# Fewer products ahead of the scores, operand loads behind a store, and a last stage entered in another order

## What is computed

```python
x = norm(x + attention0(x))   # 16 heads of dim 8, causal, distance penalty, biases
x = norm(x + experts(x))      # 8 experts, the best one for each token, 128 -> 512 -> 128
x = norm(x + attention1(x))   # 16 heads of dim 64, RMS norms on q and k, gated distance bias
x = norm(x + ffn(x))          # the last stage
# attention1 ends with  y = softmax(scores) @ v;  return y @ Wproj
# ffn: h = silu(x @ w1 * s1) * (x @ w2 * s2); h = gelu(h @ h1 * ..); h = gelu(h @ h2 * ..); return h @ w3 * s3
```

## Time and profile before

| | |
|---|---|
| median of three runs | 2333.69 us |
| profiled execution, as timed | 2337.64 us |
| its span | 2335.9 us |
| TensorE busy | 2102.8 us |
| VectorE busy | 1513.2 us |
| ScalarE busy | 1210.6 us |
| GpSimd busy | 778.7 us |
| TensorE's granted clock, mean | 0.944 of full speed |

### The profile page before, as it was taken

How to read it: one execution, slowest core, us unless ns; L and a number is a source line. 1 busy time by engine, 2 the same in 40 slices (tenths; PEclk the granted TensorE clock), 3 DMA queues, 4 the chain that set the end, 5 groups by cost and what they waited for, 6 DMA issues and landing times.

```text
span 2335.9 us, 33711 instructions
## 1 busy us (share of the span) xinstructions
PE 2102.8 (90%) x11360; PEld 1168.3 (50%) x11408; DVE 1513.2 (65%) x3409; ACT 1210.6 (52%) x1925; POOL 778.7 (33%) x480
## 2 busy tenths in 40 slices
PE   5899999998577999877999999999999995999998
PEld 2333333333566555544555555555555553655644
DVE  3777777773732778865887878888888843323311
ACT  2366666667344678854565556655565641223232
POOL 5000000000501211003777777777777780000000
PEclk7799999999689999976999999999999996999999
DMA  5233333111365579646666656666566666253300
GB/s 171 88 122 123 109 123 123 53 50 30 128 170 156 169 224 295 202 157 152 168 170 157 148 148 170 169 166 155 147 169 166 178 157 182 57 124 82 83 9 9
DMA packets 230043, 318.68 MB, mean 136 GB/s; under 512 B 22300, under 2 KB 152652, under 8 KB 229464
## 3 DMA queue, kind: packets, MB, share of 16 engines
q1 hardware_dynamic: 214568, 288.64, 45.1%
q0 software_dynamic: 7664, 24.39, 2.9%
q10 hardware_dynamic: 7640, 3.48, 0.5%
HBM read 176.52 MB, written 105.84 MB: 121 GB/s over the span
## 4 chain that ended last, share of the span: by engine, by line
PE 29%; DVE 16%; issue 8%; DMA 2%; SPq 0%; ACT 0%; DVEq 0%
PE ps L1242 9%; PE ps L906 4%; DVE a1mx L958 4%; PE ps L890 3%; DVE a1mx L962 3%; PE ps L860 3%; DVE a1KB L972 3%; PE ps L891 3%; PE ps L1193 3%; DVE a1QB L972 3%; DVE a1mx L955 1%; PE ps L1253 1%; PE ps L1231 1%; DMA frec<-s_rec 1%; PE ps L1230 1%
## 5 line engine op out<-in xcount | busy, mean ns | idle before, releaser
L1078 POOL TENSOR_TENSOR a1sum<-a1sum,a1prob 128x1024 f32<-128x1024 f32 (+3 forms) x256 | 489.4, 1912 | 66.5 <-ACT a1prob L1015 35.3
L1015 ACT ACTIVATE a1prob<-ps 128x512 f32<-128x512 f32 (+2 forms) x640 | 325.8, 561 | 251.6 <-PE ps L893 236.3
L461 DVE TENSOR_REDUCE a0grid<-ps 128x8 f32<-128x1024 f32 x288 | 349.2, 1222 | 137.2 <-PE ps L337 74.6
L563 ACT ACTIVATE a0prob<-ps 128x1024 f32<-128x1024 f32 x288 | 292.2, 1025 | 192.0 <-PE ps L363 96.8
L955 DVE CUSTOM_DVE_ANT_0 ps<-ps,c_mask_ij 128x128 f32<-128x128 f32 x496 | 262.6, 551 | 99.3 <-issue 97.6
L890 PE MATMUL ps<-a1QA,a1KA 69*128 69x512 f32 (+3 forms) x768 | 285.2, 379 | 3.4 <-PEq L33 3.4
L906 PE MATMUL ps<-a1prob,a1V 128*64 128x512 f32 (+3 forms) x1536 | 277.2, 504 | 0.0
L860 PE MATMUL ps<-a1KA,a1QA 68*128 68x128 f32 x744 | 240.8, 390 | 27.9 <-DVE a1mx L958 14.7
L891 PE MATMUL ps<-a1QB,a1KB 128*128 128x512 f32 (+3 forms) x768 | 264.2, 351 | 0.0
L906 PEld LDWEIGHTS ps<-a1prob,a1V 128*64 128x64 f32 x1536 | 104.2, 140 | 170.5 <-issue 143.6
L1075 POOL TENSOR_TENSOR a1sum<-a1prob 128x768 f32<-128x768 f32 x64 | 156.2, 2440 | 78.8 <-ACT a1prob L1015 76.7
(11 more groups left out here) (271 smaller groups left out, 3231.2 us busy)
## 6 DMA issues: line engine op xcount, KB each, us to landing
a1FK<-s_k SPq DMA_DIRECT2D x128, 256.0 KB
a1FQ<-s_q SPq DMA_DIRECT2D x128, 256.0 KB
s_xs<-c_zero POOLq DMA_DIRECT2D x19, 1024.0 KB, 9.1
s_q<-mqkT SPq DMA_DIRECT2D x32, 512.0 KB
s_k<-mqkT SPq DMA_DIRECT2D x32, 512.0 KB
s_v<-mv SPq DMA_DIRECT2D x32, 512.0 KB, 4.3
a1V<-s_v SPq DMA_DIRECT2D x32, 512.0 KB, 4.6
a1KA<-a1KB SPq DMA_DIRECT2D x64, 256.0 KB
```

Source lines behind the costliest of these rows:

```text
L461: dve.tensor_reduce(grid[g % 2][:, :, a:b + 1:b - a], banks(("max", k)), axis=AX.X, op=ALU.max).then_inc(s1_free, 1)
L563: act.activation(prob[:, :, a:b + 1:b - a, :], banks(("exp", q)), ACT.Exp).then_inc(p_full, 1)
L1015: act.activation(weights_of(g, u)[:, group[0]:group[-1] + 1, off:BANK], both(e, u, group), ACT.Exp).then_inc(weighed, 1)
L1078: pool.tensor_tensor(t[:, :, off:BANK], t[:, :, off:BANK], weights_of(g, u)[:, :, off:BANK], ALU.add).then_inc(summed, 1)
```

## The change

In the first attention:

- `EARLY` is 13. The last four of the 17 products come in the loop; the wait for drains ahead of the loop covers products 8 to 11.
- `high` and `low` have three buffers each, and there are three `stored` semaphores; ScalarE waits for the store of three chunks before.
- SP issues load_second(0) behind store(2), not ahead of it, and load_first(1) behind store(4), not store(3).
- ScalarE issues BK of group 0 behind its part of products 0 to 7.
- The waits for a batch's stores stand in one helper, ahead of each load.

In the last stage:

- The buffers of the reciprocals are swapped: those of chunk 0 lie where pair 29's operands were. load_rec(0) goes ahead of load_y(0), a pair earlier than before.
- The loads of chunk 2 are issued in `sync_program` behind the last pair's store, ahead of the write of its denominators and of the wait for the inversion.
- VectorE does join(1) ahead of the inversion; inversion and scale(2) come behind chunk 0's gates, join(2) behind chunk 1's.
- TensorE does project(2) at the end of loop 0, not ahead of the first hidden layer. ScalarE's root for join(2) moves to loop 1.

```diff
-    EARLY, NPROD, COL = 17, len(products), dim + 1
+    PARTS3, EARLY, NPROD, COL = 3, 13, len(products), dim + 1
...
-        high, low = ([over(f"{n}{r}", [P, 2, CHUNK], F32R) for r in range(2)] for n in ("high", "low"))
+        high, low = ([over(f"{n}{r}", [P, 2, CHUNK], F32R) for r in range(PARTS3)] for n in ("high", "low"))
...
+        def batch_stored(engine, b):
+
+            for c in range(b * seq // CHUNK, (b + 1) * seq // CHUNK):
+                engine.wait_ge(stored[c % PARTS3], 16 * 4 * (c // PARTS3 + 1))
...
             store(1)
+            batch_stored(sp, 0)
             still(sp, Q[0], "q0", 0, loaded1[0])
-            sp.wait_ge(cleared, 1)
-            load_second(sp, 0)
             for c in range(2, chunks):
                 store(c)
-                if c == 3:
+                if c == 2:
+                    sp.wait_ge(cleared, 1)
+                    load_second(sp, 0)
+                if c == 4:
                     sp.wait_ge(cleared, 2)
                     load_first(sp, 1)
...
-            for n in range(8, EARLY - 3):
-                drained(n)
+            for n in range(8, EARLY - 1):
+                if n % 8 < 2 * RING:
+                    drained(n)
...
-                if c > 1:
-                    act.wait_ge(stored[c % 2], 16 * 4 * (c // 2))
+                if c >= PARTS3:
+                    act.wait_ge(stored[c % PARTS3], 16 * 4 * (c // PARTS3))
...
-            for n in range(6, EARLY - 1):
+            for n in range(6, 8):
                 drain(n)
             act.wait_ge(cleared_first, 1)
+            batch_stored(act, 0)
             moving(act, BK[0], "k0", 0, loaded1[0])
-            for n in range(EARLY - 1, NPROD):
+            for n in range(8, NPROD):
                 drain(n)
...
+                if g == G:
+                    load_y(2)
+                    load_rec(2)
+                    load_x(2)
                 if g > 0:
                     store_den(g - 1)
...
-        rec = [[over(f"rec{r}{q}", [P, 4, CHUNK], place) for q, place in enumerate(places)] for r, places in enumerate((("QB0", "KB0"), ("QA2", "KA2")))]
+        rec = [[over(f"rec{r}{q}", [P, 4, CHUNK], place) for q, place in enumerate(places)] for r, places in enumerate((("QA2", "KA2"), ("QB0", "KB0")))]
...
+                load_rec(0)
                 load_y(0)
...
                 nc.sync.wait_ge(valued, unit(g - 1, NU - 1) + 1)
-                load_rec(0)
                 load_rec(1)
...
-                if c + 2 < steps:
+                if 2 < c + 2 < steps:
                     load_y(c + 2)
...
-                if c + 2 < steps:
+                if 2 < c + 2 < steps:
                     project(c + 2)
...
                 hidden_layer(c, 1, h2, hc)
+                if c == 0:
+                    project(2)
...
             join(0)
-            invert(B - 1)
             join(1)
-            scale(2)
...
+                if c == 0:
+                    invert(B - 1)
+                    scale(2)
+                if c == 1:
+                    join(2)
                 if c > 0:
                     end(c - 1)
-                if c + 2 < steps:
+                if 2 < c + 2 < steps:
                     join(c + 2)
...
+                if c == 1:
+                    root("in", 2)
                 if c > 0:
                     root("out", c - 1)
```

More of the change, by code:

```diff
@@ L135, in attention0 @@
         product, xT_full, high_full, low_full, v_full = sem("product"), sem("xT_full"), sem("high_full"), sem("low_full"), sem("v_full")
-        stored = [sem("stored0"), sem("stored1")]
+        stored = [sem(f"stored{r}") for r in range(PARTS3)]
         def product_bank(n):
@@ L148, in half @@
             return ps[:, 2 * (at[x] % RING) + m, :].rearrange("p (h a n) -> p h a n", h=PAIR, n=P)
+        def batch_stored(engine, b):
+            for c in range(b * seq // CHUNK, (b + 1) * seq // CHUNK):
+                engine.wait_ge(stored[c % PARTS3], 16 * 4 * (c // PARTS3 + 1))
         def load_first(engine, g):
+            batch_stored(engine, g // per)
             still(engine, Q[g % 2], "q0", g, loaded1[g % 2])
@@ L155, in load_second @@
         def load_second(engine, g):
+            if g > 0:
+                batch_stored(engine, g // per)
             still(engine, K[g % 2], "k0", g, loaded2[g % 2])
@@ L173, in part @@
             b, m = divmod(g, per)
-            if h == 0:
-                for r in range(2):
-                    engine.wait_ge(stored[r], 16 * 4 * (b + 1))
             row, to = (m * H + h) * dim, base_of(h // PAIR) + FIRST + 3 * (h % PAIR) * dim
@@ L192, in store @@
                 for r, part in enumerate((high, low)):
-                    nc.sync.dma_start(scr[name][r, :, c * CHUNK:(c + 1) * CHUNK], part[c % 2][:, n, :].bitcast(F32)).then_inc(stored[c % 2], 16)
+                    nc.sync.dma_start(scr[name][r, :, c * CHUNK:(c + 1) * CHUNK], part[c % PARTS3][:, n, :].bitcast(F32)).then_inc(stored[c % PARTS3], 16)
         def sync_program():
@@ L503, in drain @@
                     dve.wait_ge(high_full, 2 * c + i + 1)
-                    dve.scalar_tensor_tensor(low[c % 2][:, i, :], product_bank(n), (bq, bk)[i][:, 0:1], high[c % 2][:, i, :].bitcast(F32),
+                    dve.scalar_tensor_tensor(low[c % PARTS3][:, i, :], product_bank(n), (bq, bk)[i][:, 0:1], high[c % PARTS3][:, i, :].bitcast(F32),
                                              ALU.add, ALU.subtract).then_inc(low_full, 1)
@@ L557, in exponentials @@
                     act.wait_ge(at_rest, 16)
-                    for r in range(2):
-                        act.wait_ge(stored[r], 16 * 4 * chunks // 2)
+                    for r in range(PARTS3):
+                        act.wait_ge(stored[r], 16 * 4 * len(range(r, chunks, PARTS3)))
                 if g > 0:
@@ L583, in drain @@
                 i = "qk".index(kind)
-                if c > 1:
-                    act.wait_ge(stored[c % 2], 16 * 4 * (c // 2))
-                act.activation(high[c % 2][:, i, :], product_bank(n), ACT.Identity, bias=(bq, bk)[i][:, 0:1]).then_inc(high_full, 1)
+                if c >= PARTS3:
+                    act.wait_ge(stored[c % PARTS3], 16 * 4 * (c // PARTS3))
+                act.activation(high[c % PARTS3][:, i, :], product_bank(n), ACT.Identity, bias=(bq, bk)[i][:, 0:1]).then_inc(high_full, 1)
             for d, name in ((wq, "wq0"), (bq, "bq0"), (wk, "wk0"), (bk, "bk0")):
```

## The result

The kernel after takes 2299.37 us in the median (2296.6 to 2301.08), the kernel before 2334.82 beside it: 0.9846 of its time, 95% interval 0.9829 to 0.9863. The gain is 35.5 us; 41.8 were forecast, 2292.0 us in a range of 2283 to 2305. The profiled execution took 2298.16 us with a span of 2296.4, against 2337.64 and 2335.9: 39.5 us less.

What follows compares the result with a forecast made beforehand. TensorE is busy 90% of the span, so only its waits in the entry and last stage could yield: 37.8 + 4 = 41.8 us off the 2333.7 median gives 2292, range 2283 to 2305.

Steps and rivals of the forecast that it cites:

- The last stage, chunk 0: Last stage: chunk 0's inner layer starts at 1940.2, the next 42.0 us later at 1982.2; before, it started at 2020.99.
- rival 2: Last stage: chunk 3's reciprocals land after 1978, or last pair pays for scale(0) and load_rec(0); 5 to 14 lost; chance 0.20.
- rival 4: Last stage: the old wait returns, longer, at chunk 1, as scale(3) stands ahead of its gates; kernel slower; chance 0.02.
- The agreement of y(0): Last stage: y(0), queued behind load_rec(0), lands about 10 us later than before, near 1902.
- The last stage, the way there: Last stage: 6.22 us of waiting and 3.2 of slow projection go; chunk 0's inner layer starts 9.3 us earlier.
- The write of pair 31's row: Last pair: row written into a full queue, with GpSimd alternating with VectorE; cost taken as 1 us, bounds 0 and 3.
- The step that failed for y(1): Last stage: load_rec(1) issued about 1902.7, y(1) behind it; some 12.7 and 5.5 us, so 1921.
- The entry: First attention: row of maxima lands behind SP's backlog at about 85, scores start at 86; 4 us gained, bounds -1 and 11.
- the queue "first in first out from 21 us": First attention: operands cost 6.8 us each, chunk stores 1.4, in order on the busiest engines; all end at 84.
- Rival 1: Entry bound by compute: row overtakes backlog, or backlog is shorter; scores at 79 to 82, total gain 46 to 49; chance 0.15.

## Why the prediction was right, and where it missed

- **Size and sign.** The median lies 7.4 us above the forecast and inside the range; the gain was 35.5 by medians and 39.5 by spans, against 41.8. Of the 39.5, 2.4 come from the stretch that nothing changes; the two changed stretches gave 37.1, 4.7 short: 2.5 in the last stage, 2.2 in the entry.
- **The last stage, chunk 0.** From chunk 0's inner layer to chunk 1's the sum said 42.0 us and 42.2 were measured, against 71.5 before. This is 29.3 us of the gain, and each step of it was where it had been put: counted from chunk 0's inner layer, the denominators were read back after 10.9 us (11.3 said) and scale(3) was done after 38.8 (39.0). The gates came 6.4 us after that; the forecast gave 4 us of cover. The wait at chunk 1 of rivals 2 and 4 didn't arise; of rival 2 there is only what the last pair pays, 2.0 us.
- **The agreement of y(0) is luck.** It landed at 1902, as said. But this execution had the last stage's first weight issued 4.2 us earlier than before (1876.52, 1880.71), so y(0) took 4.2 us longer than the sum gives it. It cost nothing: its scaling ended at 1912.6, 7.9 us before TensorE wanted it.
- **The last stage, the way there.** Mis-sized terms, which make the 2.5 us between 37.8 and 35.3. The write of pair 31's row into a full queue cost 2.0 where 1 was taken, between bounds of 0 and 3. From the first issue of load_rec(1) (1900.03) to scale(1) (1923.30) went 23.3 us where the sum had 18.2, so the second projection started 8.3 us after the first, not 7.2. And the inner layer starts with 1.13, not 0.86. The step that failed for y(1) took 5.5 us for its issues, from y(0)'s in the kernel before; SP took 10.71. With the weights late it still took 10.45, but began 2.4 us nearer to the mark.
- **The entry.** The mechanism was right: the row behind the backlog on two engines, TensorE idle ahead of the scores, 36.05 for the first maxima (35), and a wait of 7.2 us (5 said). The scores start 2.3 us later than said in this profile (88.3 for 86), and 0.3 later in the two kernels whose clock came back by 42 us. Two terms were off: the queue "first in first out from 21 us" had a hole, worth 0.8 us, and TensorE's clock stayed at its lower level until 46 us here, with which the scores start up to 2.0 us later. A third was off and didn't count: the row was said to be negated near 73 and was at 78.9; the backlog ended later still. Nor does the row stand behind the backlog as a whole: seven eighths of it pass.
- **Rival 1** was given 0.15 because no row of before shows on which engines the row's write runs. The row's packets, the split loads and the row on the other queue answer it: it runs in sixteen parts, and two of them behind the backlog. Its number, scores at 79 to 82, is what came once the backlog was shortened.
- **Not foreseen:** that the stretch between, which nothing changes, varies by up to 8 us from one profiled kernel to the next, more than the whole entry is worth. A comparison of two single traces could not have sized the entry; marks at its end and at the last stage's start could.

Three things stay open. The two parts' gains (4.2 and 36.2) are 5 more than the whole; the intervals allow chance, and no run separates it. No run tells which of ScalarE's earlier request and the thirteen products carries the entry's own gain. And none tells why the issues of y take twice as long in the new place.

## What to carry to other kernels

Look at the DMA share while loads are in flight: a low share with a long landing can mean that their shape keeps them on few engines, as it did here. Then reordering mostly moves the backlog about, while splitting the loads by their outermost dimension removes it. A small transfer on which everything waits should have nothing queued ahead of it, neither on its queue nor on any engine that carries a part of it: it is only there when its last part is. And when a load is pulled forward under running work, price what that work itself sends through the same queue, and the clock that a short wait may cost.

## What the runs showed of the hardware

- For the same bytes and in the same window, loads of eight rows only kept 0.54 of the DMA engines busy and moved 109 GB/s; with half of them as sixteen-row loads, whose outermost dimension is 2, it was 0.22 and 66 GB/s, and in the kernel before 0.13 late in the backlog.
- SP issued twelve eight-row loads in 4.09 us, 0.34 each. Eight DMAs for the same operand, four of eight rows and four of sixteen, took 4.49, which by this leaves an estimated 0.78 for a sixteen-row one. Splitting cost the queue no time.
- A DMA of 8 KB ran as sixteen pieces of 512 bytes. With a backlog on two engines fourteen of them moved within 2.2 us of the issue, the last two some 6 us later.
- The row's two small DMAs, first in ScalarE's queue, still took 5.6 us while the backlog of SP's queue ran, and 9.1 behind it in SP's own.
- After the same wait of 2.0 us TensorE's granted clock was 0.50 (1.2 GHz) in a window of 5 us behind it in two kernels, and 1.00 (2.4 GHz) in the kernel after.
- After the wait for the first operands the clock was back at 1.00 in the window from 42 to 44 us in two kernels and still at 0.50 in two others, with the same code in this stretch; their scores start 1.0 to 2.0 us apart.
